# Four adjacency layers on one core: layer 2's product as three float32r passes, layer 3's ScalarE work reordered

## The reference

```
layer 0: 8 heads of 64: exp(-(a_s[i]-a_n[j])^2) * (adj>0), rows divided by their sums, @ features
layer 1: adj @ (x @ W) + b
layer 2: e = leaky_relu(s1[i] + s2[j] + a_b, 0.2); e = -9e15 where adj <= 0
         softmax(e, axis=1) @ (x @ fc_w + fc_b)            # values are 512 wide
layer 3: 4 heads of 128: sig = sigmoid(f1[i] + f2[j]); att = softmax of adj*sig where adj != 0
         encoder: att @ Xw, batch norm, mlp; decoder: att @ emb, W, elu, mlp
```

## Time and profile before

| | |
|---|---|
| median of 3 runs | 3706.84 us (3699.71 to 3708.7) |
| profiled execution | 3702.97 us, span 3701.1 us |
| mean granted TensorE clock | 0.963 |
| TensorE busy | 3251.3 us (88%) |
| VectorE busy | 2320.1 us (63%) |
| ScalarE busy | 1633.0 us (44%) |
| GpSimd busy | 238.1 us (6%) |
| layer 1's product | about 1210 to 1656 us |
| layer 2's attention | products from 1713 to 2233 us |
| layer 3's encoder attention | from 2269 us, scores from 2253 us |

### The profile page before, as it was taken

The page is one execution under the profiler, slowest core; times in us unless marked ns, Lnnn a source line. Parts: engine busy times, 40 slices in busy tenths (PEclk is TensorE's granted clock), DMA queues, the critical chain, the costliest instruction groups (busy, mean ns, idle before and its releaser), DMA issues. The chain is left out here.

```text
span 3701.1 us, 38125 instructions
## 1 busy us (share of the span) xinstructions
PE 3251.3 (88%) x13231; PEld 2093.6 (57%) x13231; DVE 2320.1 (63%) x3048; ACT 1633.0 (44%) x1399; POOL 238.1 (6%) x397
## 2 busy tenths in 40 slices
PE   5799999999977899995999995999999966999995
PEld 4533333333322677773454444777777835888884
DVE  5589888988865466655666554777777744122226
ACT  0288888888832111112222215787777602000002
POOL 0000000000001011110000001000000000000003
PEclk9999999999999899997999997999999988999997
DMA  7500000000013465652222216666566631876654
GB/s 278 196 16 8 16 8 15 15 8 14 7 62 106 168 250 224 240 218 109 97 96 96 96 63 243 240 239 258 225 259 233 240 105 69 356 275 262 265 221 125
DMA packets 109980, 557.02 MB, mean 151 GB/s; under 512 B 12576, under 2 KB 20995, under 8 KB 86064
## 3 DMA queue, kind: packets, MB, share of 16 engines
q1 hardware_dynamic: 90800, 431.91, 30.8%
q0 software_dynamic: 19072, 123.65, 9.2%
HBM read 363.33 MB, written 192.18 MB: 150 GB/s over the span
## 5 line engine op out<-in xcount | busy, mean ns | idle before, releaser
L518 PE MATMUL bank<-dist,hf 128*65 128x512 f32 (+2 forms) x2112 | 830.4, 546 | 64.2 <-ACT dist L480 64.2
L518 PEld LDWEIGHTS bank<-dist,hf 128*65 128x65 f32 x2112 | 277.1, 138 | 609.6 <-issue 457.1
L1345 PE MATMUL bank<-pt,HA 128*128 128x256 f32 x1936 | 504.3, 380 | 3.0 <-DMA HA<-features 3.0
L480 ACT ACTIVATE dist<-dist 128x1408 f32<-128x1408 f32 (+1 forms) x352 | 453.8, 1324 | 1.4
L985 PE MATMUL bank<-HB,pt 128*128 128x512 f32 x968 | 438.4, 594 | 0.0
L1534 PE MATMUL bank<-w,EM 128*128 128x256 f32 x1936 | 426.1, 380 | 12.2 <-DMA w<-weights 12.2
L1534 PEld LDWEIGHTS bank<-w,EM 128*128 128x128 f32 x1936 | 369.0, 191 | 62.9 <-DMA w<-weights 12.4
L1333 PE MATMUL bank<-idt,v 128*128 128x128 f32 x1936 | 304.3, 278 | 78.3 <-ACT pt L1223 50.7
L411 DVE TENSOR_TENSOR dist<-msk,sB 128x1408 f32<-128x1408 uint8 (+1 forms) x208 | 325.6, 1565 | 74.1 <-PE bank L518 65.4
L471 ACT ACTIVATE dist<-dist,neg_t 128x1408 f32<-128x1408 f32 (+1 forms) x208 | 296.3, 1424 | 145.1 <-DVE dist L411 145.1
L1345 PEld LDWEIGHTS bank<-pt,HA 128*128 128x128 f32 x1936 | 328.2, 191 | 26.7 <-DMA HA<-features 3.4
(11 more groups left out here) (153 smaller groups left out, 3707.6 us busy)
## 6 DMA issues: line engine op xcount, KB each, us to landing
w<-weights SPq DMA_DIRECT2D x44, 2816.0 KB, 9.8
weights<-pt SPq DMA_DIRECT2D x220, 512.0 KB, 3.6
al<-in_adj_cols SPq DMA_DIRECT2D x22, 1408.0 KB, 8.2
at<-in_adj_tiles SPq DMA_DIRECT2D x22, 1408.0 KB, 8.2
rows<-in_adj_rows SPq DMA_DIRECT2D x22, 1408.0 KB, 6.8
mrow<-in_adj_rows POOLq DMA_DIRECT2D x22, 1354.0 KB, 6.9
rows_low<-mrow POOLq DMA_DIRECT2D x22, 1354.0 KB, 6.0
rows<-rows_low POOLq DMA_DIRECT2D x22, 1354.0 KB, 8.5
```

Source lines behind the costliest of these rows:

```text
L480: act.activation(d[:, 0:VALID[c]], d[:, 0:VALID[c]], ACT.Exp, scale=-1.0).then_inc(p_ready, 1)
L518: mm = pe.matmul(sums_bank(hh, k)[0:FW, 0:hi - a * P], hf[hh][:, m, :], d[:, a * P:hi], start=(m == 0), stop=(m == T - 1))
L1345: t = pe.matmul(acc_t[n % 2][:, 0:P2], HA[:, m, h * D3:(h + 1) * D3], pt[n % 2][:, m, :, :].rearrange("p r n -> p (r n)"), start=(m == 0), ...
```

## The change

1. `pair_loop` writes out all eleven pairs on every engine; no hardware loop is left in it.
2. The values of layer 2 are no longer kept in `HB`. In layer 1's phase, `v_out` writes them to a small buffer `vt`, ScalarE rounds it to float32r (`vh`), VectorE forms the rest (`vl`), and GpSimd stores both to memory, after the load of the next `mrow`. `mrow`, `low` and `vt` now lie in `HB`'s space, and `HB` ends with this phase.
3. In layer 2 the two parts are loaded whole (`VH`, `VL`, three pieces each) on SyncE's queue, behind the loads of the second tile. Each group of turned weights is rounded by ScalarE (`keep_hi`), and VectorE writes the rest instead of a copy. TensorE makes three float32r passes instead of one fp32 product. ScalarE's order in the body of tile j is now keep_hi(j+1, 0), z, keep_hi 1, 2, 3, the copy of the features' transposes, keep_hi 4, 5, Exp.
4. In layer 3's encoder, ScalarE's order in a block is Exp b, Exp b+1, Exp b+2, copy b, Exp b+3, score b+4, score b+7, copy b+1, score b+5, copy b+2, score b+6, copy b+3. VectorE weighs unit u + 3 after group 1, 4, 3, 3 of unit u, by u % 4.

```diff
+SCORE_ORDER = (0, 3, 1, 2)
+WEIGH_AT = (1, 4, 3, 3)
 def pair_loop(eng, body, first=0, last=False):
-    lo, hi = int(first), PAIRS - int(last)
-    for i in range(lo):
+    for i in range(PAIRS):
         body(i)
-    with eng.Fori(lo, hi) as i:
-        body(i)
-    if last:
-        body(PAIRS - 1)
...
                     def v_out(j):
                         dve.wait_ge(proj_mm, 2 * T + j + 1)
-                        dve.tensor_tensor(HB[0:P, j, 0:D // 2], pj[0:P, 0:D // 2], vb[:, 0:D // 2], ALU.add).then_inc(part_out, 1)
+                        q = j % 2
+                        wait(dve, vh_ready, j - 1)
+                        wait(dve, vl_ready, j - 1)
+                        dve.tensor_tensor(vt[q][:, 0:D // 2], pj[0:P, 0:D // 2], vb[:, 0:D // 2], ALU.add).then_inc(vt_ready, 1)
...
+                        dve.wait_ge(vh_ready, j + 1)
+                        wait(dve, v_stored[q], 32 * (j // 2))
+                        dve.tensor_tensor(vl[q][:, :], vt[q][:, :], vh[q][:, :].bitcast(FP32), ALU.subtract).then_inc(vl_ready, 1)
...
                                 pool.dma_start(mrow[:, :], adj_rows[j + 1][:, 0:N]).then_inc(mrow_in, 16)
+                            pool.wait_ge(vl_ready, j + 1)
+                            pool.dma_start(v_hi[j], vh[q][:, :].bitcast(FP32)).then_inc(v_stored[q], 16)
+                            pool.dma_start(v_lo[j], vl[q][:, :].bitcast(FP32)).then_inc(v_stored[q], 16)
...
+                            act.wait_ge(proj_out, 2 * T + j + 1)
+                            wait(act, v_stored[q], 32 * (j // 2))
+                            act.activation(vh[q][:, :], vt[q][:, :], ACT.Copy).then_inc(vh_ready, 1)
...
                             sp.dma_start(xin[q][:, :], xs[1][j]).then_inc(x_in[q], 16)
+                            if j == 1:
+                                for k, (a, b) in enumerate(V_PARTS):
+                                    sp.dma_start(VH[:, a:b, :].bitcast(FP32), v_hi[a:b].rearrange("t p d -> p t d")).then_inc(v_in[k], 16)
+                                    sp.dma_start(VL[:, a:b, :].bitcast(FP32), v_lo[a:b].rearrange("t p d -> p t d")).then_inc(v_in[k], 16)
...
+                    def keep_hi(j, g):
+                        a, b = GROUPS[g]
+                        act.wait_ge(t_grp, NG * j + g + 1)
+                        wait(act, m_grp, NG * (j - 2) + g + 1)
+                        act.activation(ph_[j % 2][:, a:b, :], turn[g % 3][0:P, 0:(b - a) * P].rearrange("p (t n) -> p t n", n=P),
+                                       ACT.Copy).then_inc(t_hi, 1)
...
-                        dve.wait_ge(t_grp, u + 1)
-                        wait(dve, m_grp, u - 2 * NG + 1)
-                        dve.tensor_copy(pt[par(j)][:, a:b, :],
-                                        turn[g % 3][0:P, 0:(b - a) * P].rearrange("p (t n) -> p t n", n=P))\
-                           .then_inc(t_out, 1)
+                        dve.wait_ge(t_hi, u + 1)
+                        dve.tensor_tensor(pl_[j % 2][:, a:b, :],
+                                          turn[g % 3][0:P, 0:(b - a) * P].rearrange("p (t n) -> p t n", n=P),
+                                          ph_[j % 2][:, a:b, :].bitcast(FP32), ALU.subtract).then_inc(t_out, 1)
...
-                            t = pe.matmul(acc[q][0:P, :], pt[q][:, m, :], HB[0:P, m, :],
-                                          start=(m == 0), stop=(m == T - 1))
+                            pe.matmul(acc[q][0:P, :], ph_[q][:, m, :], VH[:, m, :], start=(m == 0), stop=False)
+                            pe.matmul(acc[q][0:P, :], ph_[q][:, m, :], VL[:, m, :], start=False, stop=False)
+                            t = pe.matmul(acc[q][0:P, :], pl_[q][:, m, :], VH[:, m, :], start=False, stop=(m == T - 1))
...
                         expo(b)
-                        if b > 0:
-                            keep(b - 1)
                         expo(b + 1)
                         expo(b + 2)
                         keep(b)
                         expo(b + 3)
                         if more:
-                            score(b + 4)
+                            score(b + SCORE_ORDER[0] + 4)
+                            score(b + SCORE_ORDER[1] + 4)
                         keep(b + 1)
                         if more:
-                            score(b + 5)
+                            score(b + SCORE_ORDER[2] + 4)
                         if b % 8 == 0 and b > 0:
                             ri_out(b // 8 - 1)
-                        if more:
-                            score(b + 6)
                         keep(b + 2)
                         if more:
-                            score(b + 7)
-                    keep(UNITS - 1)
+                            score(b + SCORE_ORDER[3] + 4)
+                        keep(b + 3)
...
-                            if g == 4 and u + 3 < UNITS:
+                            if g == WEIGH_AT[u % 4] and u + 3 < UNITS:
                                 weigh(u + 3)
```

More of the change, by code:

```diff
@@ L93, in build @@
     rows_low = scratch("rows_low", [T, P, N])
+    v_hi, v_lo = (scratch(f"values_{k}", [T, P, D]) for k in ("hi", "lo"))
     def sem(name):
@@ L193, in build @@
         f2 = sb(L0, "f2", [128, 2, T])
-        HB = sb(L0, "HB", [128, T, D])
+        heads_0 = ExitStack()
+        HB = sb(heads_0, "HB", [128, T, D])
         features_0 = ExitStack()
@@ L632, in build @@
             srow = sb(ph, "srow", [T, P])
-            mrow = sb(ph, "mrow", [P, N])
-            low = sb(ph, "low", [P, N // 4])
+            space = HB[:, :, :].rearrange("p t d -> p (t d)")
+            mrow, low = space[:, 0:N], space[:, N:N + N // 4]
+            vt = [HB[:, 8 + q, :] for q in (0, 1)]
+            vh, vl = ([sb(ph, f"{n_}{q}", [P, D], F32R) for q in (0, 1)] for n_ in ("vh", "vl"))
+            vt_ready, vh_ready, vl_ready, v_stored = sem("vt_ready"), sem("vh_ready"), sem("vl_ready"), sems("v_stored")
             mrow_in, low_ready, mrow_ready, mrow_stored = (sem(k) for k in ("mrow_in", "low_ready", "mrow_ready", "mrow_stored"))
@@ L710, in v_out @@
                         dve.tensor_copy(f2[0:P, 1, bass.ds(j, 1)], pj[0:P, D // 2 + 1:D // 2 + 2]).then_inc(part_out, 1)
-                        dve.tensor_tensor(HB[0:P, j, D // 2:D], sc[0:P, 0:D // 2], vb[:, D // 2:D], ALU.add).then_inc(proj_out, 1)
+                        dve.tensor_tensor(vt[q][:, D // 2:D], sc[0:P, 0:D // 2], vb[:, D // 2:D], ALU.add).then_inc(proj_out, 1)
+                        dve.wait_ge(vh_ready, j + 1)
+                        wait(dve, v_stored[q], 32 * (j // 2))
+                        dve.tensor_tensor(vl[q][:, :], vt[q][:, :], vh[q][:, :].bitcast(FP32), ALU.subtract).then_inc(vl_ready, 1)
                     def rest(j, q, half):
@@ L773, in _ @@
                     for q in (0, 1):
+                        pool.wait_ge(v_stored[q], 32 * PAIRS)
                         pool.wait_ge(xn_stored[q], 16 * 2 * PAIRS)
@@ L798, in build @@
         L1.close()
+        heads_0.close()
         with ExitStack() as ph:
@@ L804, in build @@
             pr = [sb(ph, f"pr{q}", [P, NP]) for q in (0, 1)]
-            pt = [sb(ph, f"pt{q}", [P, T, P]) for q in (0, 1)]
+            ph_, pl_ = ([sb(ph, f"{n_}{q}", [P, T, P], F32R) for q in (0, 1)] for n_ in ("p_hi", "p_lo"))
+            VH, VL = sb(ph, "VH", [P, T, D], F32R), sb(ph, "VL", [P, T, D], F32R)
+            V_PARTS = [(0, 4), (4, 12), (12, T)]
+            v_in = [sem(f"v_in{k}") for k in range(len(V_PARTS))]
+            t_hi = sem("l2_t_hi")
             stage, xw_stored = [sb(ph, f"stage{q}", [P, D]) for q in (0, 1)], sems("xw_stored")
@@ L850, in body @@
                             j = 2 * i + q
-                            ahead = not (isinstance(i, int) and j + 2 >= T)
-                            if ahead:
-                                z(j + 2, q)
-                            if not (isinstance(i, int) and j == 0):
-                                tail(j - 1, 1 - q)
-                            if ahead:
+                            for g in range(NG):
+                                if j + 1 < T:
+                                    keep_hi(j + 1, g)
+                                if g == 0 and j + 2 < T:
+                                    z(j + 2, q)
+                                if g == 3 and j > 0:
+                                    tail(j - 1, 1 - q)
+                            if j + 2 < T:
                                 expo(j + 2, q)
@@ L861, in _ @@
                         expo(j, j)
+                    for g in range(NG):
+                        keep_hi(0, g)
                     pair_loop(act, body, first=True, last=True)
@@ L984, in mul_group @@
                         for m in range(a, b):
-                            t = pe.matmul(acc[q][0:P, :], pt[q][:, m, :], HB[0:P, m, :],
-                                          start=(m == 0), stop=(m == T - 1))
+                            for k, (lo, _) in enumerate(V_PARTS):
```

(13 more changed lines are left out.)

## The result

| | before | changed |
|---|---|---|
| median | 3707.77 us (3699.71 to 3715.16, 4 runs) | 3656.33 us (3645.72 to 3662.65, 4 runs) |
| ratio | | 0.9861, 95% interval 0.9842 to 0.9879 |
| profiled execution | 3702.97 us | 3645.72 us |
| span, mean granted clock | 3701.1 us, 0.963 | 3643.9 us, 0.954 |

A forecast was written before the change was run, and what follows sets the result against it. Layer 2 was taken as bound by TensorE's and the row load's loops in turn, layer 1 by a store-and-load loop, the encoder by instruction order. -48 -5 -7 +4 +4 +2 -3 = -53 us, giving 3654 us, range 3618 to 3690.

The forecast's parts named there:

- Encoder, -48: Layer 3's encoder: the new order shortens four units from 31.63 to 29.2 us, over twenty blocks -48 us.
- rival (a): Encoder: its order gains only 15 to 25 us, as with a drain behind the table load; 3682 us, chance 0.17.
- reaches the fourth's at 2.67: Encoder block: VectorE starts the fourth unit's weighing 2.67 us after the block's first transposes begin, its Exp at 5.98.
- Layer 2's tiles, -5: Layer 2's attention: 19 tile periods go from 23.87 to 23.6 us with float32r passes, together -5 us.
- second loop: Layer 2: Exp, row load's issue, landing, row processing, next Exp; forecast 23.5 us, deciding in every tile.
- first loop: Layer 2: Exp, TensorE's transposes and products, copy, masked maximum, bias, next Exp; forecast to fall from 23.57 to 21.8 us.
- Rival (d): Layer 2: TensorE's idle time keeps the clock at its lower level throughout, period 35 us; 3880 us, chance 0.04.
- Layer 1, +4: Layer 1: two more GpSimd stores of 0.53 us ahead of the normalization's power cost 0.2 per tile, +4 us.
- The start of layer 2: Layer 2's start: value parts load ahead of the third row, moving its Exp from 1733.42 to 1738, +4 us.
- the last two tiles: End of layer 2: with no row to load, 44 products save 0.157 us each, -7 us.
- the way to the first Exp: Between layer 1 and layer 2's first Exp: the last value stores delay the next layer by +2 us.
- rival (b): Layer 2: the row load hides and TensorE's loop decides at 21.8 us, -40 instead of -5; 3619 us, chance 0.10.

The follow-up runs named there:

- a3_scaled: Changed kernel with GpSimd's scaling multiply in the encoder moved one unit later; 3647.77 us, ratio 0.9842 to the kernel before.
- b2_weigh: Changed kernel with every encoder weighing back after the fifth group of transposes, ScalarE's new order kept; 3743.35 us, ratio 1.0093 to the kernel before.
- a4_rows: Changed kernel with layer 2's row load issued a tile earlier, ahead of SyncE's wait for the residual sum; 3635.06 us, ratio 0.9807 to the kernel before.
- a1_loops: Kernel before with only its pair loops written out on every engine; 3700.59 us, ratio 0.9980 to the kernel before.
- b3_rows_before: Kernel before with loops written out and layer 2's row load a tile earlier, still fp32 and the old encoder order; 3695.95 us, ratio 0.9957.
- d1_fill: a4_rows plus twelve unused transposes of the identity before TensorE's wait for each tile's Exp after the first; 3624.41 us, ratio 0.9779 to the kernel before.
- b1_stores: Changed kernel with GpSimd's two value stores moved behind the next normed tile's store; 3653.95 us, ratio 0.9842 to the kernel before.
- a2_product: Changed kernel with layer 3's encoder back in its old order; 3688.90 us, ratio 0.9959 to the kernel before.
- e1_two_rows: Changed kernel with two buffers for layer 1's prepared row, next row's load ahead of the store; 3611.97 us, ratio 0.9739 to the kernel before.

## Why the prediction came out right

The total came within 3 us of the forecast partly by luck: layer 2's tiles gave some 18 us more than their term, of which the loops' 10 stood in another, and the encoder 8.5 and layer 1 6.8 less than theirs, so the errors cancel.

**Encoder, -48: right mechanism, a cost left out.** The block by ScalarE's order was worked out as 29.2 and is 29.22. The table load took 1.28 with the Exp 0.02 behind it (2606.56, 2607.86), so rival (a)'s drain isn't there. What failed is the step "VectorE ... reaches the fourth's at 2.67, and the Exp starts at 5.98": its 2.97 for the weighing holds only while GpSimd is quiet. Moving it to the second group put the fourth unit's, in every other block, beside the scaling multiply. Over the twenty blocks that the forecast counted, from the second block's first Exp to the last block's, the gain is 41.3 us in the changed kernel (632.5 to 591.3) and 47.8 in a3_scaled (584.7): with the multiply away, the forecast's 48. The rest is the first block, which the forecast took as unchanged: from the encoder's first product to the second block's first Exp it took 14.8 before and 16.6 in the changed kernel. Both halves of the order are needed (b2_weigh).

**Layer 2's tiles, -5: mis-sized, and the mechanism right in seven tiles of 19.** The step said that the second loop decides in every tile at 23.5: 6.6 to the load's issue, 7.0 to land, 9.89 to the Exp. It decides in the seven at full clock; in the other twelve, with one exception at the start, TensorE's loop does, lengthened by the fallen clock. Measured were 6.05, a landing of 6.4 in the median, and 9.66 in the tile of 22.11 (rows taken up at 1804.07, Exp at 1813.73): together 22.1. The first loop, 21.8 by the forecast, is 21.30 (a4_rows). Of the 2.27 below the 23.57 before, 0.24 are the loops' (a1_loops) and 2.03 the passes' (b3_rows_before), where 1.8 were counted. The written-out loops gave 10.1 here, while the text gave them 3 over the whole kernel. And one cost was far larger than allowed: idle time before the first transposes was given 0.3 for slower transposes; the granted clock stays low for some 3 us of passes, 1.58 per tile that has it. Rival (d) named the clock as a danger and its place rightly; the clock returns to full speed within each tile, so it costs 13 us in a4_rows (419.6 less d1_fill's 406.2) and not 230.

**Layer 1, +4: the wrong part of the loop.** The cost was sought in two issues of 0.53. These are worth a few us at most (b1_stores). What differs between the two traces is the number of late landings: GpSimd waited over 9 us for its store once in before (11.06) and three times in the changed kernel (10.34, 9.16, 10.25), and each such wait delays the normalization's power queued behind it and so TensorE. Without value stores there were one (before), one (a1_loops) and two (b3_rows_before), with layer 1 at 461.4 to 462.8; with them three (changed), one (a2_product), four (a3_scaled), two (a4_rows), one (b2_weigh), two (d1_fill) and four (b1_stores), with layer 1 at 466.7 to 482.1. That the stores' traffic makes them more frequent fits this and is not shown, as the counts overlap; what makes a landing late stays open. That the wait for them is the cost is shown (e1_two_rows).

**The rest.** The start of layer 2 (+4, measured 4.9), the last two tiles (-7, -5.7) and the way to the first Exp (+2, +1.8) held. (18 MB at 385 GB/s from 1680 on and 9.9 to the Exp make 1737, a us less than the recorded 1738; the term is hardly touched.) Of the signs given in advance, the encoder's period came out in every other block, and TensorE's waits there for the ScalarE copy went from 48.6 us to 8.6. VectorE's wait for rows stood ahead of the mask in every tile, but it had done so before too (3.54 us in the tile of the earlier trace rows), so it doesn't show that the load decides. About 4 us of idle TensorE per tile did not come out: it was 2.4 in the mean, since the tile was 1 us shorter than forecast and the fallen clock stretched TensorE's work. Layer 1's tile, forecast at 20.1 to 20.7, was 20.8 in the mean from store to store. Layer 2 ran at 22.6, halfway between the forecast's 23.6 and rival (b)'s 21.8.

## What to carry to other kernels

Moving an instruction for one engine's sake puts it beside other work of another: look at what GpSimd does in the new place of a VectorE instruction before a duration is carried over. Where one wait on a queue (here for a store to land) stands ahead of a small instruction that TensorE needs, a second buffer can be worth more than a faster product: here the whole change gave 51 us, that buffer another 44 (40 in layer 1's stage). After TensorE's work is made shorter, look for the idle time that this opens, and what the clock does behind it.

## What the runs showed of the hardware that was not expected

- VectorE's weighing (two inputs of 128x2708, 2.97 us) grew nearly by the time in which GpSimd's multiply of 128x1024 (2.38 us) ran over its start: 0.11, 0.71 and 0.99 us for overlaps of 0.24, 0.84 and 1.12. Copies out of PSUM beside the same multiply didn't grow (0.68).
- The granted clock fell behind only 2.10 us of idle TensorE, in eight of the last 18 tiles of a4_rows, and in none of d1_fill's when twelve transposes (1.47 us) stood in the gap, though 0.80 us of idle time stayed.
- Hardware loops cost 0.24 us per tile where TensorE's loop decides in layer 2 (23.57 against 23.33), and 0.54 in the mean of the 19 tiles (23.87 against 23.33), since the row load also went out 0.6 to 0.9 later and decided in some tiles.
- GpSimd's wait for a store of 1354 KB, mostly 4.7 to 6.5 us, was 9 to 11 us now and then.
- ScalarE's next instruction started 0.01 us behind the end of each of the 41 table loads in the encoder of the kernel before.
